# ScalarE takes a slot's filler one slot later in a differential-attention block on one Trainium2 core

## The reference, cut to what matters

```python
# x: (4, 1024, 128); 8 heads, each with two score maps of dimension 32, values of 64
x = x + attn(layernorm(x));  x = x + ffn(layernorm(x))
# attn:
q = (x @ Wq) ... * D**-0.5;  k, v = split(x @ Wkv)
attn_w = softmax(q @ k^T)                        # 16 maps of 1024 x 1024 per batch
attn_w = attn_w[:, :, 0] - lam * attn_w[:, :, 1] # two maps make one
attn = attn_w @ v;  attn = gamma * attn / (rms(attn) + eps) * (1 - LAMBDA_INIT)
return attn @ Wout
# ffn: 16 gated experts make q, k, v of 64; causal attention over 256 tokens; experts again
```

## Time and profile before

| what | value |
|---|---|
| median of 3 runs | 1520.96 us (1519.29 to 1521.52) |
| profiled execution, its own time | 1519.09 us |
| its span, first to last instruction | 1517.3 us |
| attention slots: first exponential to the end of the last | 37.7 to 1118.5 us |
| looped iterations (slots 32 to 223) | 163.9 to 984.7 us |
| granted TensorE clock, mean over the span | 0.970 |

### The profile page before, as it was taken

The page is one execution under the profiler, slowest core; times in us unless marked ns, Lnnn a source line. Parts: engine busy times, 40 slices in busy tenths (PEclk is TensorE's granted clock), DMA queues, the critical chain, the costliest instruction groups (busy, mean ns, idle before and its releaser), DMA issues. The chain is left out here.

```text
span 1517.3 us, 26450 instructions
## 1 busy us (share of the span) xinstructions
PE 1259.6 (83%) x8370; PEld 745.9 (49%) x8370; DVE 1266.5 (83%) x2033; ACT 1038.6 (68%) x1871; POOL 1107.2 (73%) x715
## 2 busy tenths in 40 slices
PE   3788888888888888888888888888874179999997
PEld 1444444444444444444444444444433179889887
DVE  5898999989998999999999899999986557766664
ACT  2887777777777777777777777777754155555553
POOL 3898888888888888888888888888882443434320
PEclk9899999999999999999999999999996589999999
DMA  4231111111211111111211111111003377777670
GB/s 111 71 81 48 47 29 48 29 47 39 58 34 47 35 39 47 28 48 39 55 35 47 32 43 47 28 30 27 0 1 56 68 129 119 133 117 135 115 125 10
DMA packets 184565, 86.32 MB, mean 57 GB/s; under 512 B 150176, under 2 KB 166048, under 8 KB 184480
## 3 DMA queue, kind: packets, MB, share of 16 engines
q1 hardware_dynamic: 184480, 85.33, 26.4%
HBM read 7.68 MB, written 2.10 MB: 6 GB/s over the span
## 5 line engine op out<-in xcount | busy, mean ns | idle before, releaser
L1207 DVE TENSOR_REDUCE negmax<-score_ps 128x1 f32<-128x1024 f32 x512 | 618.7, 1216 | 87.1 <-PE score_ps L584 85.3
L900 ACT ACTIVATE prob<-score_ps,negmax 128x1024 f32<-128x1024 f32 x512 | 571.6, 1116 | 128.8 <-DVE negmax L1207 116.7
L480 POOL TENSOR_TENSOR prob<-prob 128x1024 f32<-128x1024 f32 x256 | 604.2, 2360 | 21.3
L584 PE MATMUL score_ps<-ka,qa 128*128 128x512 f16 x1024 | 312.4, 387 | 119.5 <-ACT prob L900 106.0
L478 POOL TENSOR_SCALAR prob<-prob,ccol 128x1024 f32<-128x1024 f32 x256 | 287.3, 1122 | 103.9 <-DVE ccol L1220 103.5
L607 PE MATMUL trans_ps<-ident,prob 128*128 128x128 f32 x2048 | 283.3, 276 | 7.4 <-POOL prob L480 3.0
L613 PE MATMUL attn_ps<-probT,v_sb 128*64 128x512 f32 x1024 | 276.6, 620 | 1.1 <-DVE probT L322 1.1
L607 PEld LDWEIGHTS trans_ps<-ident,prob 128*128 128x128 f32 x2048 | 239.5, 142 | 75.5 <-DVE probT L322 17.7
L532 POOL TENSOR_TENSOR xs<-xnT,rw_all 128x2048 f32 (+1 forms) x32 | 115.5, 3611 | 170.4 <-DVE prob L1352 163.7
L584 PEld LDWEIGHTS score_ps<-ka,qa 128*128 128x128 f16 x1024 | 72.4, 98 | 277.9 <-ACT prob L900 234.0
L322 DVE COPY probT<-trans_ps 128x512 f32<-128x512 f32 x256 | 173.9, 679 | 2.4 <-PE trans_ps L607 2.4
(11 more groups left out here) (193 smaller groups left out, 1355.8 us busy)
## 6 DMA issues: line engine op xcount, KB each, us to landing
qa<-split SPq DMA_DIRECT2D x256, 64.0 KB, 2.0
ka<-split SPq DMA_DIRECT2D x256, 64.0 KB, 2.0
xg<-xnT SPq DMA_DIRECT2D x16, 512.0 KB, 3.0
resid<-in_L_attn_x SPq DMA_DIRECT2D x4, 512.0 KB, 5.6
wg<-in_L_attn_Wkv SPq DMA_DIRECT2D x32, 64.0 KB, 1.9
out<-yo SPq DMA_DIRECT2D x32, 64.0 KB, 2.5
wg<-in_L_attn_Wq SPq DMA_DIRECT2D x16, 64.0 KB, 1.9
xsT<-prob SPq DMA_TRANSPOSE x64, 4.5
```

Source lines behind the costliest of these rows:

```text
L480: pool.tensor_tensor(prob1[:, u, :], prob1[:, u, :], prob2[:, u, :], ALU.add).then_inc(mix_ok, 1)
L584: mm = pe.matmul(score_ps[:, sub, kh * HALF:(kh + 1) * HALF], qa[:, par, head * 2 + sub, q0:q0 + P], ka[:, par, head * 2 + sub, kh * HALF: ...
L900: act.activation(prob2[:, s % 4, :] if sub else prob1[:, s % 4, :], score_ps[:, sub, :], ACT.Exp, bias=negmax[:, s % 2, sub:sub + 1], accu ...
L1207: dve.tensor_reduce(negmax[:, s % 2, sub:sub + 1], score_ps[:, sub, :], AX.X, ALU.max, negate=True).then_inc(max_ok, 1)
```

## The change

ScalarE's handling of the filler is moved. Before, in slot s it handled the filler of slot s, after the second exponential. After, in slot s it handles the filler of slot s-1, between the first exponential and the copy of the transposed bank. The other engines' orders are not touched. The same instructions are issued as before.

```diff
                     if s < SLOTS:
                         softmax(0)
-                    copy_probT(act, act_copy, s, n, it, 0, first, last)
-                    if s < SLOTS:
-                        softmax(1)
-
-                    half = half_at(s, COPY_LAG, first, last)
-                    if half is not None:
-                        act.wait_ge(pv_ok, 8 * (4 * it + half + 1))
-                        if not (first and half == 0):
-                            act.wait_ge(rows_ok, 4 * it + half)
-                        act.activation(attnT[:, :], attn_ps[:, :], ACT.Copy).then_inc(attnT_ok, 1)
-
-                    fill = misc_fill(s, first, last)
+                    fill = None if first and s < 1 else misc_fill(s - 1, first, last)
                     if fill and fill[0] in PARTS:
                         part, step = fill
                         proj_copy(part, 2 * it + step, step % 2, "first" if first and step == 1 else "later", misc_ps[:, :])
...
                         act.activation(attn_nT[:, :, :].rearrange("p t q -> p (t q)"), misc_ps[:, :],
                                        ACT.Copy).then_inc(attn_nT_ok, 1)
+
+                    copy_probT(act, act_copy, s, n, it, 0, first, last)
+                    if s < SLOTS:
+                        softmax(1)
+
+                    half = half_at(s, COPY_LAG, first, last)
+                    if half is not None:
+                        act.wait_ge(pv_ok, 8 * (4 * it + half + 1))
+                        if not (first and half == 0):
+                            act.wait_ge(rows_ok, 4 * it + half)
+                        act.activation(attnT[:, :], attn_ps[:, :], ACT.Copy).then_inc(attnT_ok, 1)
 
                     if last and s - LN2_SLOT - 3 in range(EARLY):
                         ln2_squares(s - LN2_SLOT - 3)
```

## The result

The changed kernel takes 1504.24 us at the median (1500.37 to 1507.05, four runs), the kernel before 1520.12 beside it: ratio 0.9895 [0.9868, 0.9921]. It is faster, but by 16 us where 38 were forecast, and the time lies 2 us outside the predicted range. The profiled execution took 1505.53 us; its span is 1503.7 with a mean granted clock of 0.943 [before: 0.970], and the attention slots end at 1104.2 us instead of 1118.5. What comes after them takes 399.5 us, before 398.8.

The account below looks back on a forecast made before the run. A chain over several engines sets the pace, POOL's own work from unit 12's coefficient on. 24 groups x 1.16, edges 3.7, first and last iteration 6.7, tail -0.2 make 38.0 us: 1483 us, range 1463 to 1502.

Parts of the forecast that it names:

- The rows term: Slots 4 and 12: first exponential ahead of the row copies brings unit 12's coefficient forward, 1.0 us per eight slots.
- E0: First of a slot's two exponentials on ScalarE (L900); in slots 4 and 12 it was to begin 1.23 us earlier.
- The cols term: Slots 0 and 8: the next slot's E0 begins earlier, gaining 0.16 us per eight slots, passed on by PE.
- The later filler slots: Slots 4 to 7, 12 to 15: maxima gain about 2.0 us, lost again in slots 15 and 16; priced at nothing.
- The lock: DVE operations with both inputs in SBUF wait until POOL's running operation ends: L1232 1.3 us, attn_n again held.
- The rival without a lock: POOL lets DVE in, so the 2.03 us won by slot 15 would last: 1456 us; chance 7%.
- The edges (0.74 each) and the ends: Earlier exponential in slot 1 behind five loop edges, 0.74 us more each; first and last iteration gain 6.7 us together.
- The tail: Slot 40's cols copy comes about 1.0 us later, mostly hidden by POOL's scaling: 0.2 us lost.
- the main term: The 1.0 us per eight slots from E0 preceding the row copies; 0.89 and 1.19 were its lower and upper ends.
- Half the gain: PE's transposes, waiting for POOL's mix or a bank, hold back the first score product; 19 us left, 1502; chance 14%.
- Slower: Copies ahead of E1 cost 0.47 us per row slot if PE's queue sets the scores' start: 1536 us; chance 6%.
- E1: Second of a slot's two exponentials on ScalarE (L900); in slot 12, 0.47 us later than it could be.

Follow-up runs that it names:

- scores twice: Changed kernel, but PE computes the first score product of the next unit two times in slots 0 and 8 of 16: 1495.14 us.
- thrice: Changed kernel, but PE computes the first score product of the next unit three times in slots 0 and 8 of 16: 1478.73 us.
- more v: Kernel before the change, with the value products of one slot in eight issued twice: 1527.14 us.
- less v: Value products of one slot in eight left out: 1521.39 us on the changed kernel, 1545.63 on the kernel before.
- projections alone late: Kernel before the change, with only the q, k and v fillers taken one slot later by ScalarE: 1515.51 us.
- less v before: Kernel before the change, with the value products of one slot in eight left out: 1545.63 us, ratio 1.0188.

## Why the prediction was wrong, point by point

- **The rows term (1.0 per group): right**, 1.09 alone. E0(12) ahead of the filler, S0(13) no longer in the way of M0(13), POOL's pause gone.
- **The cols term (0.16): right in kind**, 0.11.
- **"The later filler slots … Priced at nothing": the step that failed.** Its time was right: alone they gain 0 in a full-clock group. But the step followed the 2 us that E0, S0 and the maxima win up to slot 15 only to the place where POOL's chain eats them on DVE. It did not ask where *PE* stands then. PE shares the lead, finds the "cols" transposes waiting for a DVE that is held in attn_n, and idles 2.27 instead of 1.35 us. The row for that idle was there in the trace of before (38.4 us at L657) and was left out of account. Here it costs the clock of what comes behind it: 24 falls x 1.25 = 30 us.
- **The lock: right in all it was used for.** L1232 at 1.30 at the median (0.17 at the least), attn_n at 2.40 (0.69 at the least), as the prediction had them, and both end with POOL's add. The rival without a lock (1456, a group of 31.8) is out: 32.77.
- **The edges (0.74 each) and the ends: too small.** Without the falls the looped iterations shrink by 820.8 - 785.9 = 34.9 us, against 27.8 + 3.7 = 31.5, and the middle groups account for 24 x 1.18 = 28.3 of it, so 6.6 for the edges; 1.5 of these are the fall of before behind an edge, which is gone. First and last iteration gave (1118.5 - 1073.6) - 34.9 = 10.0 instead of 6.7, of which 1.35 are the other fall of before.
- **The tail (0.2): 0.7** in the changed kernel (399.5 against 398.8).
- **The sum.** Forecast 38.0; without the falls 44.9 us at the end of the attention and 42.5 between the medians. With them 14.3 and 15.9. So the walk was 4.5 us short between the medians, and the missing term is 30.6 us at the end of the attention. (What follows the attention takes 402 to 403 us with the scores twice or thrice or more v, 406 with less v, and 396 to 399.5 in all others; why is open.) The bounds of the sum don't follow either: with 0.89 and 1.19 for the main term and the ends of the tail it gives 34.6 to 42.8, not 34.5 to 44.
- **The rivals.** "Half the gain" (1502) names nearly the measured time, but not its reason: it had PE's transposes hold back S0(13), and S0(13) is not held, as M0(13) without idle shows. "Slower" put the copies on E1's path; E1(12) starts at 889.06, 0.46 after its maximum ended (887.38 + 1.22), as the walk had it, and the group's length shows nothing of that, since S0(13) did gain.
- **The signs named beforehand.** ScalarE's copies without a wait, L1232 1.3, attn_n 2.4, POOL's pause gone: seen. DVE's idle for scores fell by 34 us in the changed kernel and by 62 with the scores thrice, where some 55 were named. "Eight slots in 32.9 on average": 811.38 / 24 = 33.8 in the changed kernel, and 785.92 / 24 = 32.7 with the scores thrice.

What stays open: the changed kernel falls in eleven of twelve middle groups with an idle of 2.26 us, the kernel with the projections alone late in three of twelve with the same idle, and less v before in five of twelve with 2.37. The length of this one idle stretch is then not all that counts. The trace of the changed kernel has a hint. Its falls follow each other at 34.13 us, while a group with a fall takes 34.02, so in the loop each begins a little later behind its idle stretch than the one before: the first run of them from 0.2 us after the idle's end up to 1.5, the second from 0.8 to 1.5. Behind the 1.5, both times, two groups have no fall. When the idle stretch comes seems to count beside how long it is; no run here varied that by itself.

## What to carry to other kernels

When a change lets an engine run ahead, follow its lead to the end: it becomes idle time somewhere, and on TensorE one longer idle stretch can cost most of what the change earns, since the granted clock can fall behind it. So read the granted clock and TensorE's idle by stretch, not by mean over the span, and try the parts of such a change one by one: here one kind of filler moved gave nearly twice the gain of all. Where the lead can't be used, products that nobody needs in the slot of the long wait, off the path, can bring the clock back, as they did here.

## What the runs showed of the hardware

- With one idle stretch of PE per group ahead of "cols", none of the twelve middle groups fell at 0.4 to 1.4 us (eight kernels), 6 at 1.83, 11 at 2.26 (but 3 with the projections alone late), 5 at 2.37 and all 12 at 3.27. A fall is 3.4 us at 0.50; it costs the group 1.25 us in the changed kernel, 0.89 with the projections alone late and 0.83 with less v before.
- Less work can be slower and more work faster on the same engine: taking 1.0 us of products per group away cost 27 us on the kernel before (18.6 in the attention), adding 30.37 - 29.52 = 0.85 us per group won 25.5 on the changed one.
- A 128x8 product on DVE takes 0.17 us when POOL rests and 1.3 or 2.1 when it meets POOL's add, 0.02 to 0.03 us beyond the add's end; attn_n 0.69 and 2.40.
